# Global attention: queries in blocks of 256, row maxima 17 steps ahead, first blocks' maxima earlier on GpSimd and SP

## What is computed

```
q = (x @ Wq).reshape(b, s, 32, 8)          # 32 heads of 8 for q and k
k = (x @ Wk).reshape(b, s, 32, 8)
v = (x @ Wv).reshape(b, s, 16, 16)
q = rope(q) * 8 ** -0.5; k = rope(k)
probs = softmax(q k^T)                      # [b, 32, 1024, 1024]
w = probs[:, even heads] - lam * probs[:, odd heads]
attn = w v, then an RMS norm over the 16 features of each head, and @ Wo
```

## Time and profile before

| | |
|---|---|
| median of 3 runs | 8156.35 us (8153.01 to 8161.66) |
| the profiled execution | 8150.33 us |
| its span, first to last instruction | 8145.2 us |
| mean granted TensorE clock | 0.959 of full speed |
| PE busy, share of the span | 7508.5 us, 92% |
| DVE | 6885.6 us, 85% |
| ACT | 6208.0 us, 76% |
| POOL | 3537.0 us, 43% |

### The profile page before, as it was taken

How to read it: one execution, slowest core, us unless ns; L and a number is a source line. 1 busy time by engine, 2 the same in 40 slices (tenths; PEclk the granted TensorE clock), 3 DMA queues, 4 the chain that set the end, 5 groups by cost and what they waited for, 6 DMA issues and landing times. The chain is left out here.

```text
span 8145.2 us, 163210 instructions
## 1 busy us (share of the span) xinstructions
PE 7508.5 (92%) x64448; PEld 2698.0 (33%) x64448; DVE 6885.6 (85%) x8962; ACT 6208.0 (76%) x11230; POOL 3537.0 (43%) x4675
## 2 busy tenths in 40 slices
PE   6899988999889998899988999889998899989999
PEld 4322343223432234322343223432234322343223
DVE  5799768997689976899768997689976999669996
ACT  3599755997569975699756997569975699656996
POOL 4256233652336623355233662345513456134661
PEclk9899988999899998999998999999999999999999
DMA  0121101221012200121001210022200222002210
GB/s 31 48 47 44 29 12 49 47 47 24 12 54 44 47 23 12 55 47 44 21 12 56 47 44 22 9 58 46 48 21 7 62 43 48 23 4 63 45 44 25
DMA packets 591392, 297.66 MB, mean 37 GB/s; under 512 B 477238, under 2 KB 515638, under 8 KB 590582
## 3 DMA queue, kind: packets, MB, share of 16 engines
q1 hardware_dynamic: 590588, 286.82, 14.5%
HBM read 123.83 MB, written 67.37 MB: 23 GB/s over the span
## 5 line engine op out<-in xcount | busy, mean ns | idle before, releaser
L1459 DVE TENSOR_REDUCE mall<-ps 128x1 f32<-128x1024 f32 x4096 | 4662.3, 1212 | 80.7 <-PE ps L1396 80.0
L1544 ACT ACTIVATE work<-ps 128x512 f32<-128x512 f32 x8192 | 4335.7, 598 | 177.9 <-PE ps L1411 33.6
L1425 PE MATMUL ps<-work,vbuf 128*32 128x256 f32 x32768 | 2620.7, 392 | 58.6 <-ACT hh L1550 58.6
L1396 PE MATMUL ps<-kop,qop 48*128 48x512 bf16 x8192 | 2521.0, 386 | 46.8 <-DVE mall L1459 25.9
L1411 PE MATMUL ps<-qop,kop 51*128 51x512 bf16 x8192 | 2511.7, 384 | 24.6 <-DMA qop<-mT 13.7
L1425 PEld LDWEIGHTS ps<-work,vbuf 128*32 128x32 f32 x32768 | 654.0, 108 | 1727.8 <-issue 1001.7
L1411 PEld LDWEIGHTS ps<-qop,kop 51*128 51x128 bf16 x8192 | 512.9, 93 | 1783.4 <-ACT work L1544 1657.5
L1484 POOL TENSOR_TENSOR mall<-mall 128x16 f32<-128x16 f32 x512 | 113.9, 222 | 1772.8 <-DVE mall L1459 1752.8
L251 POOL TENSOR_TENSOR rstd<-rstd,nhalf 128x8 f32<-128x8 f32 x64 | 109.3, 1708 | 1637.8 <-DVE rstd L245 1637.8
L443 POOL TENSOR_TENSOR hh<-work,hmask 128x1024 f32<-128x1024 f32 x256 | 521.2, 2064 | 452.2 <-POOLq L1648 331.1
L1510 POOL TENSOR_TENSOR work<-work,none 128x16 f32<-128x16 f32 x224 | 650.6, 2904 | 18.2
(11 more groups left out here) (179 smaller groups left out, 8666.0 us busy)
## 6 DMA issues: line engine op xcount, KB each, us to landing
qop<-scratch SPq DMA_DIRECT2D x512, 64.0 KB
scratch<-work SPq DMA_DIRECT2D x32, 768.0 KB, 4.2
scratch<-hh SPq DMA_DIRECT2D x32, 768.0 KB, 3.6
kop<-scratch SPq DMA_DIRECT2D x256, 96.0 KB
vbuf<-in_x SPq DMA_DIRECT2D x9, 2048.0 KB, 8.3
qop<-scratch SPq DMA_DIRECT2D x512, 32.0 KB
kop<-scratch SPq DMA_DIRECT2D x256, 64.0 KB
out<-x SPq DMA_DIRECT2D x64, 256.0 KB, 2.1
```

The costliest lines, as they stand in the source:

```text
L1396: pe.matmul(ps[:, b + n, :], qop[r:r + KQ, s, i, t * P:(t + 1) * P], kop[r:r + KQ, s, i, half(n)], start=True, stop=True).then_inc(s_ms, 1)
L1425: mm = pe.matmul(ps[VW * i:VW * (i + 1), OB, cols], vp[:, b, t, (G * gl + i) // 2, :], prob[:, u % PS, i, cols], start=t == 0 and part == ...
L1459: v.tensor_reduce(mall[:, m // CUT % 2, to, col:col + 1], ps[:, b:b + NB, :].rearrange("p b n -> p (b n)"), AX.X, ALU.max).then_inc(s_mr, 1)
L1544: act.activation(prob[:, u % PS, hl, :], ps[:, EB[slot % len(EB)], :], ACT.Exp, scale=scale).then_inc(s_ex, 1)
```

## The change

The queries of a group are cut into QB = 4 blocks of 256 instead of two of 512, and AHEAD becomes 17. With it:

- An exponent product becomes two matmuls of 256 columns with the weights of two neighbouring key tiles, written to the two halves of the same bank; ACT's exponential stays at 512 columns (two key tiles, 256 queries). `values` takes one key tile of 256 queries per step; the accumulators of two blocks in turn are the halves of the one bank. The output is kept per block (128x256), so twice as often, and PE still waits for every earlier copy.
- The maxima go per 8 reduces (CUT = 8) through `cut`, the transposing DMA and the placing: twice as many of each, of half the size. AHEAD is CUT + 9 instead of CUT + 7. SP's `maxima` stands at the step of the cut (PLACED) and no longer 3 steps later; `operands` follow the third of the four blocks.
- The early normalisation is split: its first 4 instructions (JOINED) stay, the other 10 come 8 steps later (`early_rest`); SP's transposes of the output have steps of their own (TURNED).
- At the start POOL cuts block 0 between the rotation of the last unit and its remainder. SP does stores of unit 2, `maxima(0)`, stores of unit 3, `maxima(1)`, and only then waits for the stores to land. ACT takes the four copies of the second sequence's v around the casts of the last unit, two ahead of the first pair of casts and two ahead of the second pair, and its wait for the last unit's stores moves from ahead of the first exponential to ahead of the first kept output (`project_done`).

```diff
-            def project_pool(pool):
+            def project_pool(pool, between):
...
                         for c in range(2):
                             step(pool, i, c)
+                            if i == UNITS - 1 and step is rotated and c == 1:
+                                between(0)
...
                 for i in range(UNITS):
                     order = (1, 0) if i < BY_BOTH else (0, 1)
+                    if i == UNITS - 1:
+                        kept(1, (0, 1))
                     for c in order:
                         act.wait_ge(s_ra[c], i + 1)
...
                     if i == BY_BOTH:
-                        kept(0)
+                        kept(0, range(T // 2))
+                    if i == UNITS - 1:
+                        kept(1, (2, 3))
                     for c in order:
                         act.wait_ge(s_r1[c], i + 1)
                         act.copy(part[i % 2][:, c, 1, :], rest[i % 2][c]).then_inc(s_c2[c], 1)
-                kept(1)
+                for c in range(2):
+                    act.wait_ge(s_c3[c], UNITS - 1)
+
+            def project_done(act):
                 for c in range(2):
                     act.wait_ge(s_c3[c], UNITS)
...
-            CUT = STEPS // NB
-            AHEAD = CUT + 7
-            TURN = 3
+            CUT = STEPS // QB
+            UB = CUT // 2
+            AHEAD = CUT + 9
...
-            EARLY = [STEPS * g + o for g in range(FIRST) for o in (24, 40)]
-            PLACED = [CUT * (h + 1) - 1 + TURN - AHEAD for h in range(NB * GROUPS)]
-            LATE = [STEPS * (FIRST + 1) + o for o in (16, 20)]
+            HQ = N // QB
+            TURNED = [STEPS * g + o for g in range(FIRST) for o in (19, 35)]
+            EARLY = [STEPS * g + o for g in range(FIRST) for o in (22, 38)]
+            PLACED = [CUT * (h + 1) - 1 - AHEAD for h in range(QB * GROUPS)]
+            LATE = [STEPS * (FIRST + 1) + o for o in (19, 23)]
...
                     for g in range(1, SLOTS):
                         operands(g)
+                    project_sp(sp, 2)
+                    maxima(0)
+                    project_sp(sp, 3)
+                    maxima(1)
                     for i in (2, 3):
-                        project_sp(sp, i)
                         projected_sp(sp, i)
                     for e in CLOCK:
-                        if e in EARLY:
-                            turn(EARLY.index(e))
-                        if e in PLACED:
+                        if e in TURNED:
+                            turn(TURNED.index(e))
+                        if e in PLACED and PLACED.index(e) >= 2:
                             maxima(PLACED.index(e))
...
-                        if k % STEPS == 0:
-                            pe.wait_ge(s_md[s], placed(k // STEPS))
+                        if k % (NB * CUT) == 0:
+                            pe.wait_ge(s_md[s], placed(k // (NB * CUT)))
                         bank = bank_for(k)
-                        pe.matmul(ps[:, bank, :], kop[r:r + KM, s, i, t * P:(t + 1) * P],
-                                  qop[r:r + KM, s, i, half(n)],
-                                  start=True, stop=True).then_inc(s_sc, 1)
+                        for part in range(2):
+                            mm = pe.matmul(ps[:, bank, part * HQ:(part + 1) * HQ],
+                                           kop[r:r + KM, s, i, (t + part) * P:(t + part + 1) * P],
+                                           qop[r:r + KM, s, i, quarter(n)], start=True, stop=True)
+                        mm.then_inc(s_sc, 1)
...
-                        if e == PLACED[0]:
+                        if e == 0:
                             pe.wait_ge(s_ve, TT // 2)
...
-                    project_pool(pool)
+                    project_pool(pool, cut)
                     for e in CLOCK:
-                        if at(e, 0) is not None:
+                        if at(e, 0) is not None and at(e, 0) >= 1:
                             cut(at(e, 0))
...
-                    def keep_output(u):
-                        g, n = u // (NB * T), u // T % NB
-                        act.wait_ge(s_pv, 2 * (u + 1))
-                        act.copy(oT[:, g % NG, half(n)], ps[:, OB, :]).then_inc(s_oe, 1)
+                    def keep_output(h):
+                        if h == 0:
+                            project_done(act)
+                        act.wait_ge(s_pv, 2 * UB * (h + 1))
+                        act.copy(oT[:, h // QB % NG, quarter(h % QB)],
+                                 ps[:, OB, quarter(h % 2)]).then_inc(s_oe, 1)
```

More of the change, by code:

```diff
@@ L38 @@
 PARTS = 3
+QB = 4
 Q_ROWS = [(0, 0, 1), (1, 0, 1), (2, 0, 2), (4, 1, 2)]
@@ L126, in build @@
         qf = qop[:, :, :, :].rearrange("p s i n -> p (s i n)").bitcast(F32)
[L128 to L129 removed]
+        mall = sb("mall", [P, 2, T // QB, P // 2])
+        mT = sb("mT", [P, T // QB, P], U16)
         s_w = sem("s_w")
@@ L1126, in project_pool, with kept @@
                             step(pool, i, c)
+                            if i == UNITS - 1 and step is rotated and c == 1:
+                                between(0)
             def project_act(act):
-                def kept(b):
+                def kept(b, pairs):
                     act.wait_ge(s_vz, 2)
-                    for t in range(0, T, 2):
+                    for t in (2 * i for i in pairs):
                         act.wait_ge(s_vj, T * b + t + 2)
@@ L1327, in tile_due, with quarter, closed @@
                 u = (e - 3 - part) // 2
-                return u if (e - 3 - part) % 2 == 0 and 0 <= u < GROUPS * NB * T else None
+                return u if (e - 3 - part) % 2 == 0 and 0 <= u < GROUPS * QB * UB else None
+            def quarter(n):
+                return slice(n * HQ, (n + 1) * HQ)
+            def closed(e):
+                u = tile_due(e, 1)
+                return u // UB if u is not None and u % UB == UB - 1 else None
             with nc.Block() as block:
@@ L1352, in maxima @@
                         if h >= 1:
-                            sp.wait_ge(s_md[(h - 1) // NB % SLOTS], placed(h - 1))
+                            sp.wait_ge(s_md[(h - 1) // QB % SLOTS], placed(h - 1))
                         sp.dma_start(mT[:, :, :], mall[:, h % 2].rearrange("p t c -> p (t c)").bitcast(U16), transpose=True).then_inc(s_tm, 16)
@@ L1357, in maxima @@
                             r0, k = ROWS * side + KQ, PARTS * G * side + 1
-                            sp.dma_start(qop[r0:r0 + PARTS, s, :, half(n)],
+                            sp.dma_start(qop[r0:r0 + PARTS, s, :, quarter(n)],
                                          mT[k:k + PARTS * G:2, :, :].bitcast(BF16).rearrange("c t n -> c (t n)")).then_inc(s_md[s], 16)
-                        if n == NB - 1 and SLOTS <= g + SLOTS - 1 < GROUPS:
+                        if n == QB - 2 and SLOTS <= g + SLOTS - 1 < GROUPS:
                             operands(g + SLOTS - 1)
@@ L1421, in values @@
                             if t == 0 and u >= 1:
-                                pe.wait_ge(s_oe, u // T)
+                                pe.wait_ge(s_oe, u // UB)
                         for i in range(G):
-                            mm = pe.matmul(ps[VW * i:VW * (i + 1), OB, cols], vp[:, b, t, (G * gl + i) // 2, :],
-                                           prob[:, u % PS, i, cols], start=t == 0 and part == 0, stop=t == T - 1,
+                            mm = pe.matmul(ps[VW * i:VW * (i + 1), OB, kept], vp[:, b, t, (G * gl + i) // 2, :],
+                                           prob[:, u % PS, i, cols], start=t == 0, stop=t == T - 1,
                                            skip_group_check=True)
@@ L1493, in planes, with linked @@
                             pool.tensor_copy(plane16[u], src[:, :, u]).then_inc(s_pl, 1)
-                    def early(j):
-                        done = [LINKS * j]
+                    def linked(done):
                         def link(ins):
@@ L1503, in link, with early @@
                             pool.wait_ge(s_ch, done[0])
+                        return link
+                    def early(j):
+                        link = linked([LINKS * j])
                         pool.wait_ge(s_to, 32 * (j + 1))
@@ L1512, in early, with early_rest @@
                                                 ALU.mult))
+                    def early_rest(j):
+                        link = linked([LINKS * j + JOINED])
                         pair = enrm.rearrange("p (v c) d -> p v c d", c=2)
@@ L1528, in _ @@
                             early(EARLY.index(e))
-                        if tile_due(e, 1) is not None and tile_due(e, 1) % T == T - 1:
-                            if tile_due(e, 1) // T < NB * FIRST:
-                                planes(tile_due(e, 1) // T)
+                        if e - CUT in EARLY:
+                            early_rest(EARLY.index(e - CUT))
+                        if closed(e) is not None and closed(e) % 2 and closed(e) // 2 < NB * FIRST:
```

(5 more changed lines are left out.)

25 lines of the change are left out of this document (12 added, 13 removed).

## The result

The changed kernel takes 8101.94 us (median of 4 runs, 8098.0 to 8105.31) against 8154.76 for the kernel before in the same series, 53 us less. The record estimates the ratio from the runs of both as **0.9942 (95% interval 0.9925 to 0.9958)**, which is 34 to 61 us less; the two medians alone give 0.9935. The forecast was 69 less.

The account below looks back on a forecast made before the run. DVE was taken as the bound at 1.132 us a step, PE 0.025 behind. Tail 6.6, closes 1.0 and front 1.0 make 8.6 us a pair, 69 for eight: 8087 us from the 8156.4 median, range 8045 to 8145.

Parts of the forecast that it names:

- Faster, by the lead: Tail of each pair: lead 23 to 17 removes six steps of 1.11 us, 6.6 us off.
- In-order starts: Rival, PE's middle steps: a half product delays the maxima product behind it by 0.107 us; about 8455 us, chance 0.11.
- The closes: PE's wait for ACT's accumulator copy: stall 0.33 us each 16 steps becomes 0.12 each 8, with copies of 0.37.
- 1.0 regained: Closes in the middle: of 1.6 us a pair reaching DVE, 0.6 stays and 1.0 is won back.
- level: Middle, eight steps with a close: PE needs 9.06 us and DVE 9.05, so 0.01 per block comes through.
- DVE sets the pace: Steady state of the kernel before: DVE bounds at 1.132 us a step, PE only 0.025 us behind.
- The front: First blocks of each pair: DVE's idle time falls from 3.6 to 2.6 us, 1.0 off.
- The 0.9 us behind the table load: Front: the fourth exponent product waits for ACT until 1362.6, so the 19th reduce starts 0.9 us late.
- The 1.3 of a late second block: Front: block 1's placing ends at 1371.6, PE wants it at 1370.3, a stall of 1.3 us.
- The rival of the front: Front: block 1 comes 3 to 5 us late and PE falls to low clock; 8110 to 8130, chance 0.17.
- Later blocks: SP's and GpSimd's work per block after the front lies beside DVE, with no wait; costed at nothing.
- SP is late: Rival, SP's work for each block: 64 blocks x 8 pairs late by 0.5 us, 8340 us, chance 0.03.

Follow-up runs that it names:

- e2b: Changed kernel with the maxima 23 steps ahead again, GpSimd's normalisation two steps later and operand loads after the fourth block: 8146 us, ratio 0.9998 to the kernel before.
- e4: Changed kernel with ACT's last two casts ahead of the third and fourth value copies, table load between the casts: 8092 us, ratio 0.9929 to the kernel before.
- e3: Changed kernel plus four unread float32 matmuls in PE's wait for operands before the stage's first maxima product: 8100 us, ratio 0.9936 to the kernel before.
- e8: Changed kernel with the maxima 15 steps ahead instead of 17 and GpSimd's normalisation two steps later: 8166 us, ratio 1.0006 to the kernel before.

## Why the prediction was right or wrong

- **Faster, by the lead: right.** Six steps, 6.6 us a pair forecast, 6.57 measured, in every pair; e2b takes this away again (27.9), and with it the whole gain.
- **In-order starts: refuted.** Half products stand 0.11 apart, with a maxima product at the first's start; the step is 1.110, not 1.21, a little better than the 1.117 taken. The Trainium skill ("TensorE: Matmul & The Clock Gate", Part 3, "The mechanism") has matmuls start in program order; the trace differs with it: in the middles of all eight pairs 99.8% of the maxima products start some 6 ns behind a half product and 0.11 us ahead of the next one.
- **The closes: the step that failed.** "1.0 regained" a pair became 1.3 lost, which puts the forecast 18 us off over eight pairs. The stall of 0.12 was right (0.11), the copy 0.37 was right. What was mis-sized is the price of a close, which has a second part: the exponent product held up by ACT, 0.11 more, before as after. From the middle's distances a close cost 16 x 1.1363 - 16 x 1.107 = 0.47 us before and costs 8 x 1.1391 - 8 x 1.110 = 0.23 now. Half the price, twice as often: nothing is regained. And the "level" was no level: PE needs 9.11 for eight steps against DVE's 9.05, so each nanosecond of the split counts, 0.003 x 447 = 1.3 us a pair, which is the loss. It was so before, too: 18.18 for sixteen steps against 18.10. "DVE sets the pace" held only between closes.
- **The front: mechanism half right.** The 0.9 us behind the table load came as forecast (0.88), and e4 takes it away. The 1.3 of a late second block did not: PE never waits there for the placing; its operands stood in time for a PE that was late itself. In its place came steps at the low clock, which the forecast's 2.6 of the front after the change doesn't hold. In the second pair the values are 1.08 us long there instead of 0.64:

```profile
1356.66 1.08 PE L1451 MATMUL ps<-work,vbuf 128*32 128x256 f32 x8
...
1358.64 1.08 PE L1451 MATMUL ps<-work,vbuf 128*32 128x256 f32 x8
```

  DVE's gaps behind them are 0.78, 0.76 and 0.33, 1.9 in all. So it is luck that, in pairs without a low clock from the start, the excess fell from between 5.4 and 5.9 to between 4.7 and 4.9, about the 1.0 forecast. What the steps left out besides is the low clock from the first maxima product on, 6.3 to 7.1 us in each of three pairs. The rival of the front named PE's low clock with a late block as its cause; the runs show the wait before the stage.
- **Later blocks: nothing, as costed** (no gap of DVE over 0.4 us from the 65th reduce on), but with little cover. By e3, e4 and e8 the block behind an operand load has about 1 us or less, so "SP is late" lies near.
- **The sum** was 69, all of it in the stage; the stage gave 37. The 49 us between the two profiled executions hold 12 from elsewhere, which code outside the stage also gives and takes between runs of unchanged code there (below).

## What to carry to other kernels

Ask of a buffer that is handed over whether the price of one handing over falls by more than their number grows, and take that price from the whole cycle, the second late step included, not from the first stall. An engine that is idle 0.02 us a step is no cover if it must catch up within a block. Where orders are written by hand, a lead, the queues' step numbers and the loads between them are one thing: change the lead and look at who stands ahead of whom.

## What was not expected of the hardware

- **The clock at the start of the stage.** In 9 kernels with PE's wait for operands, 12 of 72 fronts had a mean grant of 0.53 to 0.55 over the first 18 us. The wait ahead of them was 2.44 to 3.19 us in these 12 and 1.8 to 2.6 in the other 60. In the five kernels that put work into the wait, none of 40 fronts was below 0.93. A long wait goes ahead of the fall; among equal waits the runs don't show what decides.
- **Time outside the stage.** Its sum is 3203 to 3231 us in thirteen of the fourteen profiled executions, which have the same code there or nearly so (e3 has 3241), since the stretch between two stages takes 388 to 398 us, differently in each pair. The stage's own sum shows an edit of a few us where the whole time can't.
